# Weighting a batch's values one slot behind its products in a graph attention kernel

## What is computed

```python
q, k, v = feat @ Wq.T + bq, feat @ Wk.T + bk, feat @ Wv.T + bv      # each (n, 8, 32)
score = clip(einsum('ehd,ehd->eh', q[dst], k[src]) / sqrt(32), -10, 10)
ex = exp(score - segment_max(score)[dst])
alpha = ex / segment_sum(ex, dst)[dst]
wv = segment_sum(alpha[:, :, None] * v[src], dst).reshape(n, 256)
x = feat + wv @ Wp.T + bp
h = gelu(layernorm(x, ln_g, ln_b) @ W1.T + b1) @ W2.T + b2
return layernorm_plain(feat + x + h)
```

## Time and profile before

| | |
|---|---|
| median of 3 runs | 1090.16 us (1089.64 to 1092.08) |
| the profiled execution's own time | 1090.39 us |
| its span, first to last instruction | 1088.5 us |
| PE busy | 1006.4 us, 92% |
| DVE busy | 946.6 us, 87% |
| POOL busy | 833.8 us, 77% |
| ACT busy | 659.4 us, 61% |
| gathers, 750 of them | from 80.0 to 1018.4 us |
| mean granted TensorE clock | 0.981 |

### The profile page before, as it was taken

The page is one execution under the profiler, slowest core; times in us unless marked ns, Lnnn a source line. Parts: engine busy times, 40 slices in busy tenths (PEclk is TensorE's granted clock), DMA queues, the critical chain, the costliest instruction groups (busy, mean ns, idle before and its releaser), DMA issues.

```text
span 1088.5 us, 26054 instructions
## 1 busy us (share of the span) xinstructions
PE 1006.4 (92%) x6162; PEld 630.9 (58%) x6162; DVE 946.6 (87%) x1539; ACT 659.4 (61%) x1909; POOL 833.8 (77%) x1550
## 2 busy tenths in 40 slices
PE   7997879999999999999999999999999999999896
PEld 6873335565655555555555556555555555555575
DVE  6965979999999999998999899899899888988943
ACT  3213344677667766766766776676676677567442
POOL 3468888888888888888888888888888888888300
PEclk9999888999999999999999999999999999999999
DMA  9988998889889988988888888898888889889510
GB/s 309 359 274 279 302 318 270 278 282 290 265 282 289 293 272 281 292 267 277 288 281 278 278 292 262 280 293 267 277 284 279 280 273 298 257 281 289 154 37 31
DMA packets 154847, 292.26 MB, mean 268 GB/s; under 512 B 32200, under 2 KB 92326, under 8 KB 154791
## 3 DMA queue, kind: packets, MB, share of 16 engines
q0 software_dynamic: 61536, 200.85, 58.3%
q1 hardware_dynamic: 93254, 90.77, 25.6%
HBM read 257.18 MB, written 34.34 MB: 268 GB/s over the span
## 4 chain that ended last, share of the span: by engine, by line
POOL 38%; PE 20%; issue 17%; DVE 13%; DMA 6%; ACT 4%; POOLq 1%; DVEq 0%; SPq 0%; ACTq 0%
POOL kv L397 34%; PE quad L846 6%; DVE score L1580 4%; POOL idle_rows L802 4%; DVE ev L1593 3%; DMA kv<-kv_rows,src_sb 2%; DMA agg_in<-agg_rows 2%; PE bank L458 2%; PE quad L909 2%; PE bank L478 1%; PE bank L944 1%; PE quad L458 1%; DVE prod L1573 1%; ACT hid L471 1%; PE bank L918 1%
## 5 line engine op out<-in xcount | busy, mean ns | idle before, releaser
L397 POOL DMA_INDIRECT kv<-kv_rows,src_sb x750 | 711.2, 948 | 143.2 <-issue 106.0
L1573 DVE TENSOR_TENSOR prod<-kv,quad 128x1024 f32<-128x1024 f32 x196 | 239.2, 1220 | 57.4 <-DMA kv<-kv_rows,src_sb 34.6
L1593 DVE TENSOR_TENSOR ev<-kv,bank 128x1024 f32<-128x1024 f32 x196 | 238.0, 1214 | 0.5 <-ACT ev L1174 0.5
L1580 DVE TENSOR_REDUCE score<-prod 128x32 f32<-128x1024 f32 x196 | 237.7, 1213 | 0.8
L909 PE MATMUL quad<-qwin,onehotT 32*128 32x256 f32 x1568 | 142.1, 432 | 54.0 <-DVE prod L1573 49.2
L458 PE MATMUL bank<-hT,w_sb 128*128 128x256 f32 x736 | 179.6, 387 | 0.4 <-ACT hid L466 0.4
L478 PE MATMUL bank<-w_sb,hid 128*128 128x256 f32 x736 | 174.9, 387 | 0.0
L458 PEld LDWEIGHTS bank<-hT,w_sb 128*128 128x128 f32 x736 | 137.0, 191 | 33.4 <-issue 9.5
L478 PEld LDWEIGHTS bank<-w_sb,hid 128*128 128x128 f32 x736 | 138.3, 193 | 23.1 <-issue 5.6
L909 PEld LDWEIGHTS quad<-qwin,onehotT 32*128 32x128 f32 x1568 | 62.7, 185 | 145.0 <-DVE prod L1573 75.2
L918 PE MATMUL bank<-ev,onehot 128*32 128x264 f32 x1568 | 129.6, 403 | 6.0 <-DVE ev L1593 3.0
(11 more groups left out here) (154 smaller groups left out, 1291.9 us busy)
## 6 DMA issues: line engine op xcount, KB each, us to landing
dst_rows<-edge_dstT SPq DMA_DIRECT2D x50, 256.0 KB
qwin<-q_rows SPq DMA_DIRECT2D x392, 32.0 KB
kv_rows<-kv_out SPq DMA_DIRECT2D x24, 512.0 KB, 4.5
kv<-kv_rows,src_sb POOLq DMA_INDIRECT x750
agg_rows<-acc_sb SPq DMA_DIRECT2D x98, 82.5 KB
xT_sb<-xT SPq DMA_DIRECT2D x25, 256.0 KB, 5.3
q_rows<-q_next SPq DMA_DIRECT2D x25, 256.0 KB, 3.0
xq_sb<-xT SPq DMA_DIRECT2D x25, 256.0 KB
```

Of the source, the lines that this page charges most:

```text
L397: return nc.gpsimd.indirect_dma_start(out=rows, out_offset=None, in_=kv_dram, in_offset=bass.IndirectOffsetOnAxis(ap=index, axis=0))
L1573: nc.vector.tensor_tensor(prod[:, slot % 2].rearrange("p (i c) -> p i c", c=C), kv[:, slot, :, 0:C], quad[:, :, 0:C], ALU.mult).then_inc(s ...
L1580: nc.vector.tensor_reduce(score[:, slot % 2], prod[:, slot % 2].rearrange("p (h d) -> p h d", d=HD), AX.X, ALU.add).then_inc(s_score, 1)
L1593: nc.vector.tensor_tensor(ev[:, slot % 4, :, 0:C].rearrange("p i (h d) -> p i h d", d=HD), kv[:, slot, :, C:2 * C].rearrange("p i (h d) -> ...
```

## The change

DVE's slot n did: clip of n - 1, products of n, one-hots (even slots), weighting of batch n - 2, node steps, scores of n. It now does: clip of n - 1, products of n, weighting of batch n - 1, one-hots (even slots), node steps, scores of n. The one-hots wait for one exponential more than before, the one that the weighting ahead of them has waited for already.

```diff
@@ -1553,7 +1553,7 @@
             def onehots(p, slot):
                 if exists(p - 1, PAIRS):
-                    dve.wait_ge(s_exp, 2 * p - 1)
+                    dve.wait_ge(s_exp, 2 * p)
                 if exists(p - 4, PAIRS):
                     dve.wait_ge(s_part, 2 * p - 6)
@@ -1684,10 +1684,10 @@
                         clip(n - 1, (i - 1) % SLOTS)
                     if exists(n, BATCHES):
                         products(n, i, turn)
+                    if exists(n - 1, BATCHES):
+                        weight(n - 1, (i - 1) % SLOTS)
                     if i % 2 == 0 and exists(4 * turn + i // 2, PAIRS):
                         onehots(4 * turn + i // 2, i // 2)
-                    if exists(n - 2, BATCHES):
-                        weight(n - 2, (i - 2) % SLOTS)
                     node_steps(turn, i)
                     if exists(n, BATCHES):
                         scores(n, i)
```

## The result

The changed kernel took 1252.77 us (median of 6 runs, 1248.88 to 1259.44), the kernel before 1090.04 beside it: a ratio of 1.1488 with a 95% interval from 1.1469 to 1.1506. The profiled execution took 1251.23 us, with a span of 1249.4. Slower by 15%; the forecast was 1239, which is 14%.

The account below looks back on a forecast made before the run. POOL's gathers bound the kernel at 38.5 us a turn, consumers needing 37.0. With 22 turns at 44.9 (+140), start +8 and end +1, 1090.4 + 149 = 1239 us; forecast's own range 1191 to 1263, range with the clock 1185 to 1280.

Parts of the forecast that it names:

- The walk through the turn: Steps of turn 10 followed from slot to slot in the new order: 44.9 us a turn, 7.9 above DVE's 37.0.
- the wait at the GELU: DVE's weighting of slot 5 waits 4.4 us for an exponential queued behind the GELU and two table loads.
- at slot 2: DVE's weighting waits about 2.5 us for an exponential queued behind ACT's stage and PE's sums.
- at slot 0: DVE's weighting waits 0.7 us a turn for ACT's stage and exponentials.
- the rest small: DVE's waits beyond those at the GELU, slot 2 and slot 0, within 7.9 us more a turn.
- the hold of up to 0.4: Slot 4 to 5: the 8.39 us includes up to 0.4 in which ACT waited for a weighting that is now early.
- Start and end: Turns 0 and 1 cost 8 us more, between 0 and 12.8; the end costs +1, between -1.7 and +3.
- the clock: Rival: PE's clock halves at its slot 7 wait every turn, 1.63 us each, 36 in all: 1275 us; chance 0.15.
- the ring: Closed ring of waits: DVE's weighting and products, PE's slot, ACT's stage and next exponential; 44.9 us a turn.
- Only the GELU: Rival: PE and ACT run ahead, only the GELU's 4.4 us stay, 41.4 us a turn: 1160 us; chance 0.13.
- Faster: Rival: ACT stops waiting for weightings, saving POOL's 1.9 us and one weighting of 1.1: 1087.4 us; chance 0.02.
- no change: Rival: new waits stay under 1.6 us a turn, within DVE's waits for gathers; chance 0.03.

Follow-up runs that it names:

- one-hots alone: Kernel before, with DVE's one-hots moved behind the weighting and waiting for one exponential more, weighting still two slots behind: 1140.63 us against 1089.82 (ratio 1.0469).
- the copy: Changed kernel with a copy in place of the GELU of the turns, output not the reference's: 1184.62 us, ratio to the kernel before 1.0856.
- the residual first: Changed kernel with DVE's residual of slot 5 ahead of that slot's weighting instead of behind it: 1231.59 us, ratio to the kernel before 1.1306.

## Why the prediction was right

**The bound.** That the gathers set the pace and the consumers had 1.6 us a turn to spare held: the waits for gathers vanished, POOL's wait went to 106.8 us (over 100 forecast), and in three different kernels a turn is 37.0 us plus DVE's waits for exponentials: 44.9 reckoned and 45.2 measured in the changed kernel, 40.8 and 40.8 with one-hots alone, and 42.1 (37.0 + 5.09) and 42.3 with the copy. Over all 22 turns, the turn less these waits is 37.1, 36.8 and 37.1 us in these three kernels and 37.0 with the residual first. That adds up DVE's time; what makes each exponential late is shown by the rows of ACT and by the experiments. Two readings of the prediction are slightly off and change nothing: 750 gathers have 749 distances between them, so one each 1.253 us, and the 37.0 still held about 0.5 us a turn of DVE's waits for others than the gathers.

**The walk through the turn.** It gave 44.9 us. Fifteen of the 22 turns took 44.5 to 45.2. Term by term, forecast and measured in turn 10: the wait at the GELU 4.4 and 4.12, at slot 2 2.5 and 2.33, at slot 0 0.7 and 0.78, and at slots 3 and 6, "the rest small", 0.29 and 0.39. The walk went wrong at PE: a wait of about 2.5 us ahead of slot 7 was forecast for every turn and is 1.9 to 2.1 in six and at most 0.43 in the other 16, while the waits ahead of slot 4 (1.32) and in slot 5 (2.05) were not foreseen. From PE's slot 4 (561.02) to the end of the exponentials (569.16) 8.14 against 8.39, with the hold of up to 0.4 that I had named.

**Start and end.** +8 was forecast for the start and 7.8 measured; +1 for the end and 1.2 measured. So close a hit is partly luck: the 8 was chosen between 0 and 12.8, and in the runs with the copy and with the residual first, whose turns 0 and 1 do the same work, the start took 12.4 and 9.1 us more than before.

**What was too small.** The 22 turns took 999.9 us where 988 were forecast. These 12 us lie in one term, which I had set to nothing in the forecast and kept as a rival: the clock. Seven of the turns (3, 6, 8, 13, 16, 19, 22) took 46.4 to 46.8 in place of some 45, so 45.45 on average. Six of the seven follow a slot 7 in which the clock fell. Slots 5 and 7 of turn 12, which makes turn 13 long:

```profile
661.11 0.46 PE L424 MATMUL bank<-bias_rows,one_rows 2*128 2x512 f32 x1 [2.06 <-DVE x L436]
661.50 2.86 PE L478 MATMUL bank<-w_sb,hid 128*128 128x256 f32 x12
...
670.90 1.04 PE L909 MATMUL quad<-qwin,onehotT 32*128 32x256 f32 x8 [2.08 <-DVE prod L1573]
671.87 1.12 PE L444 MATMUL bank<-ident,hn 128*128 128x128 f32 x4
672.78 2.78 PE L478 MATMUL bank<-w_sb,hid 128*128 128x256 f32 x8
675.49 0.65 PE L918 MATMUL bank<-ev,onehot 128*32 128x264 f32 x8
```

From q_rows to sums 4.59 us, to the hundredth what slot 7 of turn 13 had shown in the kernel before, against 2.96 at full clock (580.94 to 583.90 in turn 10). The place and the price of the rival were right, the frequency wasn't: six turns in 22, not every one. The reason is the wait that the walk had left out. PE waits twice, in slot 5 for the residual and in slot 7 for the products, and in each of the 22 turns the clock falls once: in slot 5 in 16 of them, in slot 7 in the six others (2, 5, 12, 15, 18, 21). Where it falls in slot 5, PE reaches slot 7 late, waits there 0.43 us at most and keeps its clock. Such a fall is nearly always free: leaving out the seven long turns, the nine with the fall in slot 5 took 44.5 to 45.2 and the six without it 44.8 to 45.1.

Turn 8, the seventh long one with 46.69, is the exception. There the lower clock lasted longer, so that the twelve matmuls of slot 5 took 5.49 in place of 4.54 and the q_rows behind them 1.07 in place of 0.71:

```profile
480.64 5.49 PE L478 MATMUL bank<-w_sb,hid 128*128 128x256 f32 x12
486.06 1.07 PE L909 MATMUL quad<-qwin,onehotT 32*128 32x256 f32 x8
```

PE then reached slot 7 with no wait left, so the rest of the delay went round the ring. What decides between slot 5 and slot 7 isn't shown: the wait in slot 5 is 1.9 to 2.1 us in every turn, with the fall behind it and without. The Trainium skill (TensorE: Matmul & The Clock Gate, Part 1) tells of the halved clock after idle stretches, with which these rows agree in that each of the 22 falls comes at the end of a wait of PE or soon behind it; that a fall at one place can spare another, costlier one is these rows' own.

**The range.** Its lower end, 1191 for turns of 43 us, was added up wrongly: 1090.4 + 98 + 9 is 1197. The measured time lies in the range either way.

**The table loads.** The pair of exponentials ended 0.37 us behind the table load of 1.28, as in the trace of before. The drain of 1.38 us that the Trainium skill (ScalarE: Activation LUTs, What ACT_TABLE_LOAD costs) gives beside it doesn't show: with it the time would have been near 1300, an estimate from the page's figure, and the copy in place of the GELU would have given back 5.3 us a turn at the wait, where 2.84 came off it.

**The other rivals.** Only the GELU (1160): the copy leaves 95 us of the loss, so no. Faster and no change: POOL's and DVE's waits speak against both. That the one-hots' move costs nothing was true in its place behind the weighting, where they waited 1.2 us in the whole run; by itself it costs 51 us, since it wants the same exponential and, in two slots, waits for the weighting in front of it.

## What to carry to other kernels

How far one engine runs behind another is the cover of everything the other has queued in between, not of the one instruction that is waited for. Before shortening such a distance, look up in the timeline, slot by slot, when the awaited result was really done against when the new order wants it; total waits don't show it, since a wait that is covered reads as nothing (0.5 us here, and 200 after). If the sum of the new waits exceeds the slack of the engine per turn, the difference is paid in every turn.

## What the runs showed of the hardware

- A memset of 0.12 us between two gathers on POOL costs nothing: the gathers start 1.25 us apart with it and without it, and with the DMA engines busy 0.88 or 0.71 of the time.
- PE at the lower clock costs nothing where PE waits afterwards for longer than it lost: nine turns with such a fall in slot 5 and no delay from the slot 7 ahead took 44.5 to 45.2, as long as turns without it, and the one in which the fall lasted longer took 46.69. Raising the mean clock from 0.956 to 0.971 gave no time of its own, since in six turns the fall stood at a place on the ring.
- The same kernel took 1090 us on some chips and 1477 to 1507 on two others, with instructions of DVE and ACT as long as ever and ACT's `stage` starting up to 3.5 us after the sums of PE (0.15 elsewhere). A difference of 13% between two orders, the residual first against the kernel before, was 1.6% there.
